# Mixture-of-experts blocks: up projection from high and low parts in single passes, down projection issued inside the next block, six one-bank buffers

## The reference, cut to what matters

```python
x = hidden_states.reshape(-1, D)                        # 4488 tokens, D = 192
probs = softmax(x @ gate_w)                             # 8 experts
top_w, top_i = top_k(probs, 2)                          # each token goes to two experts
h = gelu(einsum('td,edf->tef', x, w_up) + b_up)         # F = 768
y = einsum('tef,efd->ted', h, w_down) + b_down
out = einsum('ted,te->td', y, combine)
```

## Time and profile before

| | |
|---|---|
| Median of 3 runs | 4592.13 us (4589.54 to 4593.84) |
| The profiled execution | 4594.65 us |
| Span of its trace | 4592.5 us |
| TensorE busy over the span | 84%, 3869.3 us |
| Last scatter of `place_phase` issued | about 3994 us |
| `blocks_phase`, first up projection | 4013.05 us |
| `blocks_phase`, last `y` written | 4486.50 us |
| First gather of `combine_phase` | 4490.36 us |

### The profile page before, as it was taken

The page is one execution under the profiler, slowest core; times in us unless marked ns, Lnnn a source line. Parts: engine busy times, 40 slices in busy tenths (PEclk is TensorE's granted clock), DMA queues, the critical chain, the costliest instruction groups (busy, mean ns, idle before and its releaser), DMA issues. The chain is left out here.

```text
span 4592.5 us, 66354 instructions
## 1 busy us (share of the span) xinstructions
PE 3869.3 (84%) x21988; PEld 2541.8 (55%) x21988; DVE 2150.8 (47%) x3265; ACT 2117.4 (46%) x3304; POOL 1147.7 (25%) x1126
## 2 busy tenths in 40 slices
PE   1799999999999999999849999999999963099990
PEld 1355555555555555555436767767667743088880
DVE  2566666656666656666435444444445423011112
ACT  0355455545545544544516676566666630022220
POOL 4123323323332322332210010010000010633326
PEclk6799999999999999999969999999999985599995
DMA  6323333332433232233011111111111132455544
GB/s 134 115 79 94 114 97 91 104 101 84 97 111 95 85 114 88 78 114 101 22 43 29 25 29 38 27 29 36 27 26 38 29 102 76 94 165 153 159 130 124
DMA packets 306312, 378.52 MB, mean 82 GB/s; under 512 B 63559, under 2 KB 209415, under 8 KB 305927
## 3 DMA queue, kind: packets, MB, share of 16 engines
q1 hardware_dynamic: 258967, 284.95, 22.5%
q0 software_dynamic: 23168, 73.32, 6.1%
q10 hardware_dynamic: 24016, 18.09, 1.2%
HBM read 245.69 MB, written 101.30 MB: 76 GB/s over the span
## 5 line engine op out<-in xcount | busy, mean ns | idle before, releaser
L691 DVE TENSOR_REDUCE mx<-ring 128x2 f32<-128x1024 f32 x768 | 919.7, 1223 | 486.4 <-PE ring L478 483.1
L605 ACT ACTIVATE probs<-ring 128x1024 f32<-128x1024 f32 x768 | 767.7, 1024 | 411.9 <-PE ring L491 410.6
L1421 DVE TENSOR_REDUCE a_nmx<-a_ring 128x1 f32<-128x561 f32 (+1 forms) x480 | 341.7, 737 | 308.1 <-PE a_ring L1270 159.2
L1319 ACT ACTIVATE a_ring<-a_ring,a_nmx 128x561 f32<-128x561 f32 (+1 forms) x480 | 333.8, 695 | 196.9 <-DVE a_nmx L1421 193.9
L478 PE MATMUL ring<-k_stack,q_stack 48*128 48x512 f32 x1536 | 359.6, 479 | 55.4 <-DVE mx L691 23.2
L491 PE MATMUL ring<-q_stack,k_stack 64*128 64x512 f32 x1536 | 358.4, 484 | 54.4 <-DVE mx L691 39.5
L505 PE MATMUL acc<-probs,vals 128*32 128x512 f32 x3072 | 393.9, 633 | 1.3 <-ACT probs L605 1.3
L1200 POOL TENSOR_SCALAR_AFFINE_SELECT a_probs<-a_probs 128x256 f32<-128x256 f32 (+1 forms) x240 | 91.9, 383 | 1208.4 <-ACT a_probs L1351 1208.4
L1351 ACT ACTIVATE a_probs<-a_ring 128x561 f32<-128x561 f32 (+1 forms) x480 | 287.3, 637 | 169.4 <-PE a_ring L1267 166.5
L1267 PE MATMUL a_ring<-a_k_hh,a_q_hl 128*128 128x256 f32 (+1 forms) x960 | 310.4, 338 | 23.0 <-DVE a_q_hl L1401 11.0
L1267 PE MATMUL a_ring<-a_q_hl,a_k_hh 128*128 128x256 f32 (+1 forms) x960 | 287.4, 325 | 10.4 <-ACT a_ring L1319 7.6
(11 more groups left out here) (206 smaller groups left out, 6575.2 us busy)
## 6 DMA issues: line engine op xcount, KB each, us to landing
q_stack<-qk_scratch SPq DMA_DIRECT2D x576, 64.0 KB, 2.4
k_stack<-qk_scratch SPq DMA_DIRECT2D x576, 64.0 KB, 2.5
qk_scratch<-qk_hi SPq DMA_DIRECT2D x32, 768.0 KB, 3.7
qk_scratch<-qk_lo SPq DMA_DIRECT2D x32, 768.0 KB, 5.2
a_q_hm<-a_q_hl SPq DMA_DIRECT2D x48, 280.5 KB
a_k_hh<-a_k_hh SPq DMA_DIRECT2D x48, 280.5 KB
h_in<-tokens SPq DMA_DIRECT2D x34, 384.0 KB, 4.4
res<-tokens SPq DMA_DIRECT2D x32, 384.0 KB, 3.4
```

Of the source, the lines that this page charges most:

```text
L605: nc.scalar.activation(probs[n % 2][:, pair:pair + 2, x // 2, :], buf[:, :, :], ACT.Exp, scale=DK ** -0.5).then_inc(act, 1)
L691: nc.vector.tensor_reduce(mx[s][:, i, :].rearrange("p (r t) -> p r t", r=2)[:, :, t], buf[:, :, :], AX, ALU.max).then_inc(dve, 1)
L1319: nc.scalar.activation(buf, buf, ACT.Exp, bias=nmx[0:r, i, h:h + 1], accum_out=sums[0:r, i, h:h + 1]).then_inc(act, 1)
L1421: nc.vector.tensor_reduce(nmx[0:r, i, h:h + 1], flat(buf)[0:r, 0:N], AX, ALU.max, negate=True).then_inc(dve, 1)
```

## The change: what it does

**High and low parts.** The up projection was a product of fp32 operands. Now each operand v is split into a high part, v rounded to the reduced fp32 format (`F32R`), and a low part, v minus the high part, and the product is taken as high x high + high x low + low x high, each a matmul of the reduced format. The 192 contraction rows are cut as 128 + 64 instead of 96 + 96. The first chunk takes three matmuls. In the second chunk the upper 64 rows of the array, which would be idle, hold the high weights once more and the low inputs, so two matmuls do for it. An `up` step is five matmuls of 256 columns. ScalarE makes the high parts of the weights with three copies for each block (steps `hi`), VectorE the low parts with two subtractions (steps `lo`). VectorE splits the transposed input with two copies and two subtractions instead of the one copy.

**Order.** The steps are in a new list, `blocks_turn`. The two `down` steps of a block stand behind the next block's steps `up` 1 and `up` 2. The transpose of the next block still stands before the last two `up` steps. The first two turns and the last are written out as straight code, and eight turns are a loop.

**Buffers.** Six PSUM buffers of one bank replace three of two banks.

**DMAs.** `wup` is gathered by two indirect DMAs (128 and 64 rows of 768 elements), so a block has five. They are issued as `wup`, `wup`, `bup`, `wdown`, `bdown`. GpSimd waits for `which` alone. The store of `y` moves from ScalarE's queue to SyncE's, in front of the loads of the same place. `which` has four columns instead of three, which costs three small VectorE operations in `place_phase`.

```diff
-def block_steps():
-    out = [("t", 0)]
-    for b in range(PLACES):
-        out += [("up", b, m) for m in range(4)]
-        out += [("t", b + 1)] if b + 1 < PLACES else []
-        out += [("up", b, 4), ("up", b, 5)]
-        out += [("down", b, 0), ("down", b, 1)]
+def blocks_turn(without=()):
+    out = []
+    for b in range(PLACES):
+        prev, nxt = (b - 1) % PLACES, (b + 1) % PLACES
+        out += [("up", b, 0), ("hi", nxt, 0), ("up", b, 1), ("down", prev, 0), ("up", b, 2), ("hi", nxt, 1), ("lo", nxt, 0),
+                ("down", prev, 1), ("up", b, 3), ("hi", nxt, 2), ("lo", nxt, 1), ("t", nxt), ("up", b, 4), ("up", b, 5)]
...
+M_AHEAD = [("hi", 0, 0), ("hi", 0, 1), ("lo", 0, 0), ("hi", 0, 2), ("lo", 0, 1), ("t", 0)]
...
-        ring = [ctx.enter_context(nc.psum_tensor(f"m_ring{i}", [P, 2, 512], F32)) for i in range(RING)]
+        ring = [ctx.enter_context(nc.psum_tensor(f"m_ring{i}", [P, 512], F32)) for i in range(BUFFERS)]
...
         @block.sync
+                    await_step(sp, R, it, "dve", step, now)
+                    sp.sem_inc(tick, 1)
+                    sp.dma_start(of_block(slots_out, done * PLACES + b), y[b][:, :, :]).then_inc(stored[b], 16)
+                    if not (R is R_CLOSE or R is R_FINAL and b < PLACES - 1):
+                        load((done + 1) * PLACES + b, b)
...
         @block.gpsimd
-                    g.wait_ge(dve, C.value(it, "dve", ("down", b, 1), turns_back=1))
-                    for dst, table, k, r in ((wup[b][:, :, :].rearrange("p c f -> p (c f)"), "wup_rows", 0, KC),
-                                             (wdown[b][:, :, :].rearrange("p k d -> p (k d)"), "wdown_rows", 1, P),
-                                             (bup[b][:, :], "bup_rows", 1, P), (bdown[b][:, :], "bdown", 2, P)):
+                    for dst, table, k, r in ((wup[b][:, 0, :], rows_768, 0, P), (wup[b][0:LOW, 1, :], rows_768, 1, LOW),
+                                             (bup[b][:, :], dram["bup_rows"], 2, P),
+                                             (wdown[b][:, :, :].rearrange("p k d -> p (k d)"), dram["wdown_rows"], 2, P),
+                                             (bdown[b][:, :], dram["bdown"], 3, P)):
...
         @block.tensor
-                        for c in range(2):
-                            last = nc.tensor.matmul(buf[:, 0, 0:BLOCK], wup[b][:, c, P * m:P * m + P], xT[b][:, c, :],
-                                                    start=(c == 0), stop=(c == 1))
+                        if m == 0:
+                            await_step(pe, R, it, "act", ("hi", b, 2), now)
+                            await_step(pe, R, it, "dve", ("t", b), now)
+                        f = slice(P * m, P * m + P)
+                        for n, (w, v) in enumerate(((w_hi[b][:, 0, f], x_hi[b][:, 0, :]), (w_hi[b][:, 0, f], x_lo[b][:, :]),
+                                                    (w_lo[b][:, 0, f], x_hi[b][:, 0, :]), (w_hi[b][:, 1, f], x_hi[b][:, 1, :]),
+                                                    (w_lo[b][0:LOW, 1, f], x_hi[b][0:LOW, 1, :]))):
+                            last = nc.tensor.matmul(buf[:, 0:BLOCK], w, v, start=(n == 0), stop=(n == 4))
...
         @block.scalar
+                    if kind == "hi":
+                        n = step[2]
+                        if n == 0:
+                            sc.wait_ge(gathered[b], per_turn(R, it, 80, 160 if b == 0 else 80))
+                        dst, src = ((w_hi[b][:, 0, :], wup[b][:, 0, :]), (w_hi[b][0:LOW, 1, :], wup[b][0:LOW, 1, :]),
+                                    (w_hi[b][LOW:P, 1, :], wup[b][0:LOW, 1, :]))[n]
+                        nc.scalar.activation(dst, src, ACT.Copy).then_inc(act, 1)
...
         @block.vector
+                    if kind == "lo":
+                        v.wait_ge(act, R.done(it, "act", ("hi", b, n), now))
+                        nc.vector.tensor_tensor(w_lo[b][0:r, n, :], wup[b][0:r, n, :], w_hi[b][0:r, n, :].bitcast(F32),
+                                                ALU.subtract).then_inc(dve, 1)
+                    elif kind == "t":
+                        v.wait_ge(mm, R.done(it, "mm", step, now + 1))
+                        nc.vector.tensor_copy(x_hi[b][:, 0, :], buf[:, 0:BLOCK])
+                        nc.vector.tensor_copy(x_hi[b][0:LOW, 1, :], buf[0:LOW, BLOCK:2 * BLOCK]).then_inc(dve, 1)
+                        v.wait_ge(dve, R.done(it, "dve", step, now + 1) - 1)
+                        nc.vector.tensor_tensor(x_lo[b][:, :], buf[:, 0:BLOCK], x_hi[b][:, 0, :].bitcast(F32), ALU.subtract)
+                        nc.vector.tensor_tensor(x_hi[b][LOW:P, 1, :], buf[0:LOW, BLOCK:2 * BLOCK],
+                                                x_hi[b][0:LOW, 1, :].bitcast(F32), ALU.subtract).then_inc(dve, 1)
```

More of the change, by code:

```diff
@@ L1869, in combine_phase @@
+            with v.Fori(0, LOOPS) as it:
+                steps(R_LOOP, it)
+            for R in (R_FINAL, R_CLOSE):
+                steps(R, 0)
 def combine_phase(nc, fused, slots_out, weight, slot, out_dram):
```

192 lines of the change are left out of this document (125 added, 67 removed).

## The result

The changed kernel takes 4580.2 us (median of 20 runs, 4570.3 to 4594.7), the kernel before 4593.7 (20 runs beside it). The ratio is 0.9968, with a 95% interval from 0.9959 to 0.9977: faster by 13 to 15 us, where 65 were forecast and 4564 was the upper end of the range. The direction was right and the size was off by a factor of four to five.

A forecast was written before the change was run, and what follows sets the result against it. TensorE was taken to bound the block stage. First product at 4018.8, plus 7.1, 42 blocks of 9.1 and 13.1 gave 4421.2 against 4486.5, 65 us less: 4528 us forecast, whole range 4494 to 4564.

The forecast's parts named there:

- The 64-row matmul is counted like the full ones.: In the `up` step: the fifth matmul costs 0.1215 us like the others, so a step takes 0.61 us, six 3.65.
- the forecast's own range: Range of the main forecast: a block period of 8.8 to 9.4 us, 4515 to 4541 us, 68 in 100.
- stall at the boundary: Between blocks TensorE waits for VectorE's last subtraction of the next input: 0.9 us, making a block 9.1 us.
- wait for the Gelu: Ahead of the `down` steps: TensorE's 0.56 us wait for the last `up` step's Gelu goes.
- VectorE's four operations: Preparing the next block's input: four operations of 256 columns instead of one copy, 1.66 us together.
- The first product: At the start of the block stage: the first product comes at 4018.8 instead of 4013.05, 5.8 us later.
- a right chain: Refill of a weight place, from the last add to the fifth gather's landing: 12.7 us, where 15.5 is allowed.
- The order's part: `down` behind two next `up` steps: the 0.56 us Gelu wait goes, a 0.9 us boundary stall comes.
- rival 1: At the block boundary: VectorE's operations overlap more, the block falls to 8.2 us, the time to 4490; 8 in 100.
- rival 2: Refill of a place binds if its chain exceeds 15.5 us; at 18 us, block 9.9, time 4562; 15 in 100.
- rival 3: TensorE's clock falls to 1.2 GHz for a share of the stage; at 0.3, 4630; 5 in 100 with other slower ways.
- the rule of four passes: In the `up` step: the skill's rule gives 0.54 us instead of 0.61 and 4510 instead of 4528; the rows were taken.

The follow-up runs named there:

- `e2_pair`: Against the changed kernel, the 64-row matmul comes first in every odd `up` step, so that two stand together: 4591.6 us, ratio 0.9977.
- the padded kernel: Changed kernel with the fifth matmul of each `up` step on all 128 rows, unused weight rows zeroed: 4586.3 us, then 4519.4 us on another chip (fourth batch).
- the padded kernels of the first chip: Changed kernel with the fifth matmul on 128 rows, 4586.3 us, and the same with copies, low parts and transposes moved earlier, 4563.6 us.
- the earlier order: Padded kernel with copies and low parts of the next weights earlier and transposes ahead of `up` 3: 4563.6 us, on another chip 4528.5 us.

## Why the prediction was wrong

**The step that failed** is one sentence of the up projection: "The 64-row matmul is counted like the full ones." The rows that it leaned on the earlier trace rows hold ten matmuls of 128 rows each. There is no row in them where the number of rows changes from one matmul to the next, so the cost of a change was never bounded. Measured, each change costs 0.19 us, and an `up` step has two: 0.60 + 0.38 = 0.98 us, and six steps 5.9 instead of 3.65. The padding alone, with nothing else changed, brought the step to 0.59 and the block to 8.82, against 9.1 forecast, and the time to 4519, against 4528, within the forecast's own range. The other way round it holds too: with 0.98 us for a step the prediction's own reckoning gives 10.4 us of issue for a block and no stall at the boundary (VectorE is ready at 10.3), and some 4585 us in all (an estimate), against 4580 measured.

The kernel before had the price in its trace, just behind the last row (3003.38):

```profile
3003.83 0.30 PE L1267 MATMUL a_ring<-a_k_l,a_q_hm 128*49 128x306 f32 x1
3004.06 0.10 PEld L1270 LDWEIGHTS a_ring<-mask,eye 49*49 49x49 bf16 x1 [0.25 <-issue]
3004.06 0.20 PE L1270 MATMUL a_ring<-mask,eye 49*49 49x49 bf16 x1
```

Here a matmul of 128 rows is followed by the mask matmul with 49 rows. Between 2000 and 3700 us this happens 96 times, and the second starts 0.23 us behind the first (0.227 to 0.238). Ahead of the same mask matmul with 128 rows, 192 times, it is 0.14 (0.138 to 0.147): again 0.09 less. But not every change of rows has this price. The fp32 matmuls of the kernel before go from 128 rows to 96 and back. There the weight load is early, 0.16 us ahead of the matmul at 4240.67, and the `up` row starts 0.163 us behind the last `down` row, as `down` rows do among themselves:

```profile
4240.51 3.38 PEld L1812 LDWEIGHTS m_ring<-m_xT,m_wup 96*128 96x128 f32 x16
```

The weight load stands in the rows as the visible part: between 128 rows and 64 it is not done early. The Trainium skill, page "TensorEngine Tiling (Array Packing)", section Key Properties, says that "changing tiling mode (not just tile) drains the TensorE". If a change of rows from 128 to 64 counts as such a change, the trace agrees with it, and it puts numbers to it that the page does not have.

**From the forecast to the result**, from first product to last add, 402.4 us were forecast and 458.2 measured. Forty-two blocks of 10.30 on the mean instead of 9.1 are 50.4 of the 55.8; the first block took 10.7 instead of 7.1 us, since the clock was at 0.50 through all of it; the end, with its longer `up` steps, is 1.8 us longer. The first of the forty-two took 13.8 us, because the clock rose only in it. That late rise goes with the row changes too. The clock rose 18.4 and 17.7 us behind the first product in the two profiles of the changed kernel, 8.5 us with the order undone, 5.8 us in `e2_pair`, and 3.6 us in the padded kernel (fourth batch), whose window reads:

```profile
4020.00:4032.00 12.00, 9.41 (x69) 9.27 (x70) 5.60 (x13) 6.56 (x14) 5.34 (x6) 1.00 0.57 181
```

How the changes would hold the clock down, and whether they do so alone, is not shown.

**What held.** The `down` steps lost their wait for the Gelu. VectorE's four operations took 4208.66 to 4210.30, 1.64 us against 1.66. ScalarE's copies (0.83) and Gelus cost nothing. The first product came 5.1 us later in relation to SyncE's first issue, against 5.8. The refill cost TensorE nothing in the changed kernel, but by room and not by a right chain (15.7 us and not 12.7, just over the 15.5 that the prediction allowed for a block of 9.1: the last gather is issued 10.5 us behind the add and not 8.3, and lands after 5.0 and not 4.3). And the stall at the boundary, 0.9 us behind VectorE's last subtraction, is there in the padded kernel with 0.8 to 0.9; in the changed one the longer `up` steps covered all but 0.16 of it. That the padded block takes 8.82 and not 9.1 is a sum of small terms: TensorE needs 8.0 us with its restart and not 8.2, and most stalls are 0.81 and not 0.9. Of the 0.2, 0.1 is the `down` steps, whose 4.00 us held a restart behind the Gelu wait that went: 24 rows of 0.163 are 3.9. **The order's part was undervalued**: the forecast let the stall of 0.9 take the place of the 0.56, so for it the order gained nothing and the products everything. In the changed kernel it was the other way round. What the order is worth in the padded kernel was not tried.

**The rivals.** The boundary costing nothing (rival 1) was nearly true, but for a reason that raised the time. The refill (rival 2) did not bind here; it lengthened a few blocks of the padded kernel (9.6 to 9.9 us instead of 8.82), and bound as soon as the stream came to 8.1 us a block. The clock (rival 3) fell in the padded kernels of the first chip, to 0.88 in a window, and on other chips one to four times for 3.4 us each in five profiles of their variants (windows of 0.97 to 0.98 in the earlier order), but not in the changed kernel. Its text also named the stretch of 0.56 at the start, and the sum left it at the length that it had before: it became 13 us longer, which cost about 7 us. By the rule of four passes an `up` step would take 0.54 us, by the rows 0.61; the padded kernel's takes 0.59, nearer to the rows.

**What stays open.** What delayed TensorE's semaphore updates on the first chip: four kernels had it there, the two that were repeated on other chips had not. Whether the changed kernel itself would show it on that chip was not tried. All runs are taken with the profiler on, so whether it happens without one isn't known either. Nor was it tried whether the refill, which binds in the earlier order, could be relieved in another way than by taking a gather off GpSimd.

## What to carry to other kernels

Keep the number of rows the same in a series of short matmuls: zeros in the unused rows cost nothing here, and a change between 128 and 64 rows costs more than the matmul itself. When a price is taken from rows of the trace, check that every property that the new instruction has (rows, columns, what stands ahead of it) occurs in those rows; where it doesn't, look for it elsewhere in the trace (here it stood just behind the rows that were used), and bound it where it isn't found. When a gain is of the size of the scatter, compare the length of the changed stage in the traces, and not the whole time. And repeat a surprising control on a second chip before a theory is built on it: here four kernels were spent on a gather that had nothing to do with the matter.

## What the runs showed of the hardware

- A change from 128 to 64 rows or back between single-pass matmuls of 256 columns costs 0.19 us, more than such a matmul (0.12), and the weight load ahead of it isn't done early. Between 128 and 96 rows, in the fp32 matmuls of the kernel before, the load is early and no such gap shows.
- On one chip the updates at the end of TensorE's steps came up to 3 us late in four kernels, in bursts 0.07 us apart, while its matmuls went on; in the padded kernel 44 of 396 are missing from that trace. The same kernel took 4586 us there and 4519 on another chip, while the kernel before took 4604 there and 4593 on the other.
- TensorE's clock rose to 2.4 GHz during thirty small unread matmuls and was back at 1.2 GHz after 2.7 us without work, for another 10 us.
- An indirect gather's issue on GpSimd took 1.22 us on the median (0.90 to 1.69) in the changed kernel when a VectorE subtraction of 768 columns, with both inputs in SBUF, overlapped it by over 0.3 us, and 0.94 with none beside it: 0.28 more, where the earlier trace rows had 0.12.
- A transfer of 576 KB whose address is read from a register, on SyncE's queue, replaced an indirect gather and 1.25 us of GpSimd's time per block; with it the padded kernel in the earlier order is at 0.979 of the time before, without it at 0.985.
